# Four transformer layers in one launch: late weights in five portions, value products moved, signals by tile, a shorter quantising chain, joined layer norms, an output product that starts by tile

## The reference, cut to what matters

```python
x = x + jnp.tanh(g_xattn[0]) * _L0_xattn_ref(_layernorm(x, axis=-1), ctx_1024, ...)   # linear attention
x = x + jnp.tanh(g_ffn[0])   * _L0_ffn_ref(_layernorm(x, axis=-1), ...)               # quantised gate/up/down
x = x + jnp.tanh(g_xattn[1]) * _L1_xattn_ref(...)                                     # local attention
x = x + jnp.tanh(g_ffn[1])   * _L1_ffn_ref(...)                                       # 16 experts, 2 shared
x = x + jnp.tanh(g_xattn[2]) * _L2_xattn_ref(ctx_1024, _layernorm(x, axis=-1), ...)   # latents over the context
x = x + jnp.tanh(g_ffn[2])   * _L2_ffn_ref(_layernorm(x, axis=-1), ...)               # quantised, GELU
x = x + jnp.tanh(g_xattn[3]) * _L3_xattn_ref(...)                                     # softmax attention
x = x + jnp.tanh(g_ffn[3])   * _L3_ffn_ref(...)                                       # 8 experts
```

```python
scale = 127.0 / jnp.clip(jnp.max(jnp.abs(x), axis=-1, keepdims=True), EPS, None)
xq = jnp.clip(jnp.round(x * scale), -128.0, 127.0)
```

## Time and profile before

| what | value |
|---|---|
| time, median of 3 runs | 959.98 us (953.85 to 960.44) |
| the profiled execution: its own time | 959.54 us |
| its span in the trace | 957.6 us, so 1.9 us lie around it |
| busy in the span | PE 744.9, DVE 634.9, ACT 396.7, POOL 279.7 us |
| the chain that ended last, shares of the span | PE 40%, DVE 21%, issue 4%, POOL 3%, ACT 3% |
| the load of `d_att` in layer 0, from issue to landing (the page's DMA issues) | 2.8 us |
| moved by DMA | 93.99 MB |

### The profile page before, as it was taken

The page is one execution under the profiler, slowest core; times in us unless marked ns, Lnnn a source line. Parts: engine busy times, 40 slices in busy tenths (PEclk is TensorE's granted clock), DMA queues, the critical chain, the costliest instruction groups (busy, mean ns, idle before and its releaser), DMA issues.

```text
span 957.6 us, 16273 instructions
## 1 busy us (share of the span) xinstructions
PE 744.9 (78%) x5488; PEld 493.0 (51%) x5488; DVE 634.9 (66%) x1329; ACT 396.7 (41%) x650; POOL 279.7 (29%) x217
## 2 busy tenths in 40 slices
PE   4879759999748237699469999994259899985997
PEld 3757637777536123566235555553114566652665
DVE  3879479998865667555565556655758989925553
ACT  1556346666611102235144554550103777762431
POOL 1442142333412003025318777770032000000111
PEclk8889969999965558589799999998556999997999
DMA  6467836654232000011232224202910565610230
GB/s 183 151 209 268 257 142 196 211 191 152 81 114 20 0 0 1 1 31 69 77 77 67 67 74 126 68 1 31 157 38 22 132 157 131 173 43 22 66 99 21
DMA packets 46649, 93.99 MB, mean 98 GB/s; under 512 B 16698, under 2 KB 30010, under 8 KB 44274
## 3 DMA queue, kind: packets, MB, share of 16 engines
q1 hardware_dynamic: 46594, 93.25, 33.8%
HBM read 61.58 MB, written 31.65 MB: 97 GB/s over the span
## 4 chain that ended last, share of the span: by engine, by line
PE 40%; DVE 21%; issue 4%; POOL 3%; ACT 3%; DVEq 0%; POOLq 0%; ACTq 0%
PE ps L972 7%; DVE arena L2062 7%; PE ps L962 6%; DVE arena L1519 4%; PE ps L907 3%; PE ps L1132 2%; PE ps L1070 2%; PE ps L1142 2%; PE ps L1059 2%; ACT arena L1350 1%; POOL arena L1489 1%; PE ps L1044 1%; PE ps L920 1%; POOL arena L1430 1%; DVE arena L1534 1%
## 5 line engine op out<-in xcount | busy, mean ns | idle before, releaser
L1519 DVE TENSOR_TENSOR arena<-ps,arena 128x448 f32<-128x448 f32 (+8 forms) x160 | 99.4, 642 | 68.4 <-ACT arena L1288 20.7
L2062 DVE TENSOR_REDUCE arena<-ps 112x1 f32<-112x500 f32 x192 | 115.4, 668 | 14.0 <-PE ps L1044 13.1
L1489 POOL TENSOR_TENSOR arena<-arena 125x448 f32<-125x448 f32 x96 | 108.8, 1133 | 24.5 <-ACT arena L1327 20.8
L1430 POOL TENSOR_TENSOR arena<-arena 112x4 f32<-112x4 f32 x13 | 13.3, 1022 | 308.7 <-DVE arena L1539 308.7
L972 PE MATMUL ps<-arena 125*128 125x448 f32 (+1 forms) x208 | 97.1, 548 | 1.3 <-ACT arena L1327 0.8
L1350 ACT ACTIVATE arena<-ps 125x896 f32<-125x896 f32 x96 | 87.0, 917 | 25.9 <-PE ps L1059 25.5
L1519 DVE TENSOR_TENSOR arena<-ps,rn 125x448 f32<-125x448 f32 x96 | 59.3, 618 | 50.0 <-PE ps L962 45.2
L1327 ACT ACTIVATE arena<-arena,kbias 125x448 f32<-125x448 f32 x96 | 63.7, 668 | 65.0 <-DVE arena L1519 46.3
L671 PE MATMUL ps<-w_k2h,arena 128*125 128x512 f16 x288 | 69.7, 400 | 21.3 <-ACT arena L1213 21.1
L962 PE MATMUL ps<-arena 128*125 128x448 f16 (+3 forms) x312 | 78.0, 360 | 3.0 <-DVEq L1530 3.0
L1411 POOL TENSOR_TENSOR arena<-arena,vec 125x1536 f32<-125x1536 f32 x8 | 27.6, 3452 | 164.3 <-DVE arena L1519 164.3
(11 more groups left out here) (274 smaller groups left out, 1375.0 us busy)
## 6 DMA issues: line engine op xcount, KB each, us to landing
d_k<-arena SPq DMA_DIRECT2D x24, 375.0 KB
d_v<-arena SPq DMA_DIRECT2D x8, 1125.0 KB
arena<-d_k SPq DMA_DIRECT2D x96, 93.8 KB
arena<-d_v SPq DMA_DIRECT2D x8, 1008.0 KB
arena<-in_ctxT SPq DMA_DIRECT2D x8, 750.0 KB, 13.6
d_cln<-arena SPq DMA_DIRECT2D x8, 750.0 KB
d_clnT<-arena SPq DMA_DIRECT2D x8, 750.0 KB
arena<-d_clnT SPq DMA_DIRECT2D x8, 750.0 KB
```

Of the source, the lines that this page charges most:

```text
L1489: ins = pool.tensor_tensor(psum2[p][0:rows], psum2[p][0:rows], pexp[(t + p) % 2][0:rows], ALU.add)
L1519: return dve.tensor_tensor(out, a, b, op)
L2062: dve.tensor_reduce(mx3[bn % 2][:, u % 2, u % 8 // 2, u // 8:u // 8 + 1], ps[0:TT, max_bank_of(bn, u), 0:500], AX.X, ALU.max).then_inc(l3_ ...
```

## The change

1. `rest` is no longer issued in one go after batch 1, but in five portions, one behind each `store_results` of batches 1 to 5: `wquant`; the constants; vectors, `sel` and `kmask`; five small weights; `qks`, `b1v`, `gates` and `x`. The loop over batches on SP is written out.
2. PE's layer-1 value products move from before `wsum` to behind the product with `w_d0`. Their bias is now one product of 512 columns per parity instead of one of 64 columns per parity and batch.
3. Each product into a hidden layer counts up a semaphore of its own kind (`h_in`), so ACT and DVE start on the first tile when it is there. In the first quantised part the row maximum of a tile follows its product directly.
4. Quantising takes off the constant and clips at 127 in one instruction. The clip at -128 is gone (a row scaled by its own maximum lies within -127 and 127).
5. The two norms behind each other become one, with variance v(1+eps)+eps² under the root; POOL's `rsqrt` is called once for both.
6. PE's output product of layer 2 waits for each pair of batches, and no longer for all.

Cut to its core:

```diff
-            for b in range(2):
-                store_results(b, b)
-            for dst, src in rest:
-                sp.dma_start(dst, src).then_inc(ld_w, 16)
-            with sp.Fori(1, B // 2 - 1) as i:
-                for p in range(2):
-                    store_results(2 * i + p, p)
-            for b in (B - 2, B - 1):
-                store_results(b, b % 2, more=False)
+            portions = {1: rest[0:1], 2: rest[1:2], 3: rest[2:5], 4: rest[5:10], 5: rest[10:14]}
+            for b in range(B):
+                store_results(b, b % 2, more=b + 2 < B)
+                for dst, src in portions.get(b, ()):
+                    sp.dma_start(dst, src).then_inc(ld_w, 16)
...
-            for r in range(2):
-                for b in range(B):
-                    dst = ps[SP * r:SP * r + S, 2, 64 * b:64 * b + 64]
-                    pe.matmul(dst, c56T[:, S * b:S * b + S], head_parity(w_l1[:, 2, :], r), start=True, stop=False)
-                    mm = pe.matmul(dst, cs("mean", 1)[:, 0:S], head_parity(vec[0:1, V128.index("L1_vb"), :], r),
-                                   start=False, stop=True)
-                mm.then_inc(l1_kv, 1)
             pe.wait_ge(wsum_in, 1)
             pe.matmul(ps[0:D, 1, 0:5], cs("mean"), mw, start=True, stop=True).then_inc(wsum, 1)
             pe.wait_ge(l0_ld, 16)
             transposes(y2, 4)
             op.next()
             by_tokens(xT2, w_d0[:, :], 0)
+            for r in range(2):
+                pe.matmul(ps[SP * r:SP * r + S, 2, :], cs("mean", 1)[:, 0:S],
+                          head_parity(vec[0:1, V128.index("L1_vb"), :], r).unsqueeze(1).broadcast_to([1, B, 8, HD16]),
+                          start=True, stop=False, skip_group_check=True)
+            for b in range(B):
+                for r in range(2):
+                    mm = pe.matmul(ps[SP * r:SP * r + S, 2, 64 * b:64 * b + 64], c56T[:, S * b:S * b + S],
+                                   head_parity(w_l1[:, 2, :], r), start=False, stop=True, skip_group_check=True)
+                    if b == B - 1:
+                        mm.then_inc(l1_kv, 1)
...
                     for m in range(n_first):
-                        mm = pe.matmul(ps[0:TT, t + 4 * m, :], zqT[:, TT * t:TT * t + TT], wquant[:, first + m, :],
-                                       start=True, stop=True)
-                mm.then_inc(product, 1)
+                        pe.matmul(ps[0:TT, t + 4 * m, :], zqT[:, TT * t:TT * t + TT], wquant[:, first + m, :],
+                                  start=True, stop=True).then_inc(h_in[m], 1)
...
-            pe.wait_ge(l2_done, B + 2)
             for t in range(NT):
+                pe.wait_ge(l2_done, 2 * t + 4)
...
-                ch.link(dve.tensor_scalar(tmp, tmp, MAGIC, -128.0, ALU.subtract, ALU.max))
                 if ffn is None:
-                    dve.tensor_scalar(dst, tmp, 127.0, None, ALU.min).then_inc(operand, 1)
+                    dve.tensor_scalar(dst, tmp, MAGIC, 127.0, ALU.subtract, ALU.min).then_inc(operand, 1)
...
-            product_in.next()
             for t in range(NT):
+                dve.wait_ge(h_in[1], t + 1)
                 act_in.next()
-                ch.step(dve.scalar_tensor_tensor(big2[:, t, :], ps[0:TT, 4 + t, :], acol[:, 3, t:t + 1],
+                ch.link(dve.scalar_tensor_tensor(big2[:, t, :], ps[0:TT, 4 + t, :], acol[:, 3, t:t + 1],
                                                  big[:, t, :], ALU.mult, ALU.mult))
+                ch.step(dve.tensor_reduce(acol[:, 0, t:t + 1], big2[:, t, :], AX.X, ALU.max,
+                                          apply_absolute_value=True))
...
-            layernorm(x, z, 1e-5)
-            layernorm(z, y, 1e-5, "L2_lw", "L2_lb")
+            layernorm(x, y, 1e-5, "L2_lw", "L2_lb", twice=True)
...
-            layernorm(x, z, 1e-5)
-            layernorm(z, z, 1e-5, "L2f_g", "L2f_be")
+            layernorm(x, z, 1e-5, "L2f_g", "L2f_be", twice=True)
```

27 lines of the change are left out of this document (16 added, 11 removed).

## The result

The changed kernel takes 930.74 us in the median of 4 runs (929.24 to 932.43), the kernel before 958.88 beside it (953.85 to 960.44). The ratio is 0.9707, with a 95% interval of 0.967 to 0.9744. The profiled execution takes 930.32 with a span of 928.7, so 28.9 us of span are gone, where the sum said 40.2. The forecast of 920 was too low, and the range (914 to 929) missed the time by 1.7 us.

The account below looks back on a forecast made before the run. No one engine was taken to bound the kernel: a context-load stall, then stages where each instruction waits for the one before. Terms 17.4 + 4.0 + 4.3 + 7.6 + 3.7 + 3.2 = 40.2 off 959.54 gave 920 us, range 914 to 929.

Parts of the forecast that it names:

- Portions: Context pass: spreading the 14 weight DMAs removes the stall of batch 3 to 4; gain 17.4 us, bounds 16.3 and 17.9.
- the charge of 0.5: Context pass, batches 2 to 5: 0.5 us taken off for portions issued just behind a context load, from 0 to 1.6.
- nothing is charged: Context pass: portions ahead of the `d_cln`, `d_k` and `d_v` stores on SP cost 0, their next reader being 52 us on.
- Rival (a): Context pass: portions share the queue evenly with the load in front, 7 us of waits, 927; chance 0.13 with smaller forms.
- sentence on ring order: Context pass: engines take a ring's descriptors in order, so a portion behind a load can't delay it; gain the full 17.9.
- Rival (b): Context pass: the stall of batch 4 isn't from the weights and comes back, so 17.4 is missing: 937; chance 0.07.
- rival (c): Context pass: SP held 12.27 us at a full queue behind each of four portions, 49 against 40: 969; chance 0.02.
- Value products: Layer 0: PE's weight sum comes earlier, but DVE's scale passes alternate with POOL's key blocks; gain 4.0 us, bounds 3.8 and 6.4.
- Cover: Layer 0: moved value products and ACT's copies end at 322.3, 0.9 us before PE's next use at 323.2.
- First quantised part: Quantised part after layer 0: single passes on z and hidden layer, tile-by-tile signals; 0.5 + 1.3 + 2.5 = 4.3 us.
- The gain is the whole idle time: Output product of layer 2: three quarters begin 3.7 us earlier, PE the bound from then on; gain 3.7 us.
- the only rival on it: Whole kernel: a shorter chain leaves PE's clock higher, DVE not let down by POOL; 3 to 6 us more, 912 to 917; 0.08 below 915.

Follow-up runs that it names:

- the memset: Changed kernel plus one DVE memset of 2.3 us ahead of the norm of layer 3: 929.2 us, ratio 0.9691.

## Why the prediction was wrong

**Portions (forecast 17.4, in the trace 9.7).** The step that failed is the charge of 0.5, "as batch 3, whose load was followed by all 14 weights, showed no wait". That row tells of a load that stands ahead of the weights. But a portion that stands behind one load stands ahead of the next, and of the stores between them, for which I had written "nothing is charged". The charge was 8.0 in the trace (waits of 3.32 and 4.65). Rival (a) had the size right (7 us, 927), but not its reason, even sharing of the queue at 270 GB/s: the queue had no room since two stores of each batch used 5 engines of 16. With them split the same portions cost nothing, 105.15 us between the marks for 123.11. The prediction's sentence on ring order, by the Trainium skill (DMA: Bandwidth & Descriptors, Queues, rings and completion order), gave the full 17.9. The runs don't refute that rule: the constants stood ahead of the first load that came late, the vectors and the mask ahead of the second, and stores of 125 rows ahead of both. But I had applied it to one load and not to the next. Rival (b) was partly right as well: 7.0 of the old stall's 15.78 us go with the split stores alone. Of rival (c) the 12.27 us block came once (9.98, behind the mask), not four times. A smaller part is at the tail: from the last mark to the end it takes 41.5 instead of 39.8, and PE's granted clock there reads 0.73 from 241 to 246, where it was 1.00 throughout before; other traces have 39.8 to 42.9 for it. Even with no wait at all, as with the stores split, the end of the pass came 14.4 us earlier and not 17.4. And 1.5 of the 9.7 is luck, since the batches ahead of the stall were that much earlier.

**Value products (4.0; 5.4).** The mechanism was right: the scale passes are drawn out by POOL's blocks beside them, 7.58 us for five. It isn't what bounds the stretch, though: `d_att` lands too late for more than 1 us of it to count. "A gain of 4.0" was too small in the trace by 1.4, and part of this is luck of the clock. The old value products ran wholly at 0.50 in the profiled run before, 12.5 us; in the kernel before with split stores they took 9.3, since the clock stood at 1.00 for half of them. Against that trace, `xT2` comes only 1.1 us earlier. The forecast of 10 us for the moved products was far off: they take 3.9. Cover was 8 us and not 0.9.

**First quantised part (4.3; 4.1), joined norms (7.6; 7.5), second quantised part (3.2; 3.0).** Right, each by the steps given: 1.38 us a tile, 3.8 a norm, 1.3 for the single pass on the hidden layer.

**Output product (3.7; 5.6).** Mis-sized. "The gain is the whole idle time" left out that an idle PE comes back at the lower clock. In the kernel before, PE idles 3.74 us and takes 8.95; in the changed one it goes straight on and takes 7.20. The 3.74 cost 1.9 more than themselves. The run that puts the wait back shows both at once.

**Layers 1 and 3 and the end (0; -6.6).** The step that failed is to put the stages that the change doesn't touch at nothing. "Nothing but the missing rows speaks for the clock" left the clock out of the sum, and the only rival on it had it rise. Layer 3 with the same code takes 149.0 to 159.0 us. In the changed kernel the granted clock falls at six of its batch turns, at 1.3 us each (a batch of 17.1 instead of 15.8). The kernel before had no fall there, but lost 3.4 us against the 149.0 in uneven batches, PE's standstills among them; the difference of the two is the 4.1. When only its stores are split, the kernel before shows both, four falls and a standstill of 2.09: 159.0 for 152.4. Layer 1 isn't fixed either: its attention reads 53.4 to 55.6 in traces with the same code, 55.6 in the changed kernel's.

That neither the code of layer 3 alone nor a wait for its data sets its length is shown by the memset and by the waits. What does is open: the same short waits of PE stand at the turns in either case, and only in some traces does the clock fall behind them. Whether it goes with the kernel or with the execution is half open too. Five more traces, of this kernel and of four with the same layer 3, have the very 156.5, which speaks for the kernel; but the two traces with one memset differ by 1.3, and executions of one kernel by up to 8.7 us.

By the terms, 40.2 less 7.7 for the context pass and 6.6 for the untouched stages, and 3.4 more from the value and output products, less 0.4 for the rest, is 28.9. Had the sum been right for the context alone, the forecast would have been 927, and either miss alone would have left the time within the range.

## What to carry to other kernels

A queue that is full now and then must be priced by the engines that its transfers use, not by its bytes: look for windows in which the queue is busy and its DMA share reads only a third, and change the shape of the transfers in it before moving others around them. When a wait of PE goes, add what the clock gives back behind it, and when one is made, what it takes; read the same product in a stretch with and without idle time ahead. And where a long stage changes its length with untouched code, give every forecast a share of that (here 10 us, 1%) from the start, and judge an edit by the marks around it, not by the end.
